# A fused attention and mixture-of-experts kernel: where the padding is awaited, how routing counts are kept, and where the residual is added

## The reference

```
x = layernorm(x + attn(x))                       # x: 1 x 2048 x 128
scores = x @ Wr + br                             # 8 experts
top 2 of scores; weights = softmax over these 2
out = sum over experts i of (relu(x @ W1[i] + b1[i]) @ W2[i] + b2[i]) * weight[i]
x = layernorm(x + out)                           # W1[i]: 128 x 512, W2[i]: 512 x 128
```

## Time and profile before

| what | us |
|---|---|
| median of 3 runs (lowest, highest) | 260.19 (259.41, 263.42) |
| the profiled execution | 259.66 |
| its span | 258.0 |
| busy: TensorE, VectorE, GpSimd, ScalarE | 183.3, 149.1, 119.6, 110.9 |

### The profile page before, as it was taken

How to read it: one execution, slowest core, us unless ns; L and a number is a source line. 1 busy time by engine, 2 the same in 40 slices (tenths; PEclk the granted TensorE clock), 3 DMA queues, 4 the chain that set the end, 5 groups by cost and what they waited for, 6 DMA issues and landing times.

```text
span 258.0 us, 5886 instructions
## 1 busy us (share of the span) xinstructions
PE 183.3 (71%) x1385; PEld 147.0 (57%) x1385; DVE 149.1 (58%) x546; ACT 110.9 (43%) x345; POOL 119.6 (46%) x188
## 2 busy tenths in 40 slices
PE   2999968609887899987420879897979798992000
PEld 1556425407565667655310879797969698892000
DVE  5489937007988857777660245554545445552393
ACT  1188774203556446665310224343424333450086
POOL 5000300041717636776776246666666636665360
PEclk9999995756999689999555599999999989998555
DMA  5999999995000101101113565666555656520743
GB/s 168 269 209 205 207 208 208 178 250 167 3 0 1 35 10 44 32 32 34 41 52 104 140 199 164 195 182 180 158 172 160 181 159 163 184 68 1 225 163 102
DMA packets 39554, 33.87 MB, mean 131 GB/s; under 512 B 3807, under 2 KB 33173, under 8 KB 39521
## 3 DMA queue, kind: packets, MB, share of 16 engines
q1 hardware_dynamic: 35264, 25.68, 45.2%
q0 software_dynamic: 3312, 7.64, 8.4%
q10 hardware_dynamic: 944, 0.17, 0.3%
HBM read 19.15 MB, written 14.79 MB: 132 GB/s over the span
## 4 chain that ended last, share of the span: by engine, by line
PE 24%; issue 11%; DVE 6%; POOL 5%; DMA 3%; ACT 2%; SPq 1%; POOLq 1%; DVEq 1%; ACTq 0%
PE psum L1337 11%; PE psum L1350 10%; POOL expert_results L534 3%; ACT x_sb L722 1%; PE psum L1325 1%; DMA xg<-expert_rows 1%; DMA gate<-expert_results 1%; DVE fstats L1101 1%; DVE xT L1098 1%; DMA expert_results<-kT,dest 1%; POOL dest L530 1%; DVE fshift L1093 1%; POOL expert_rows L490 0%; SPq L399 0%; PE psum L1239 0%
## 5 line engine op out<-in xcount | busy, mean ns | idle before, releaser
L534 POOL DMA_INDIRECT expert_results<-kT,dest x39 | 38.5, 987 | 37.4 <-issue 13.8
L1064 DVE TENSOR_SCALAR gT<-psum,b_sb 128x128 f32<-128x128 f32 x78 | 23.8, 346 | 35.9 <-PE psum L1337 23.3
L1350 PE MATMUL psum<-w_sb,gT 128*128 x312 | 43.8, 285 | 0.8 <-DVE gT L1064 0.8
L1350 PEld LDWEIGHTS psum<-w_sb,gT 128*128 128x128 f32 x312 | 39.2, 197 | 2.3 <-issue 1.4
L490 POOL DMA_INDIRECT expert_rows<-xr,slot x32 | 31.6, 986 | 13.4 <-issue 11.1
L699 ACT ACTIVATE gT<-psum,b_sb 128x128 f32<-128x128 f32 x78 | 24.4, 364 | 18.1 <-issue 15.1
L689 ACT ACTIVATE kT<-psum 128x128 f32<-128x128 f32 x39 | 10.8, 278 | 48.0 <-PE psum L1325 38.6
L1337 PE MATMUL psum<-kT,km 128*128 128x128 f32 x168 | 24.2, 292 | 9.1 <-issue 9.1
L1337 PEld LDWEIGHTS psum<-kT,km 128*128 128x128 f32 x168 | 22.0, 205 | 10.1 <-issue 10.1
L470 POOL TENSOR_TENSOR km<-kT,ek 128x512 f32<-128x512 f32 x4 | 5.1, 1282 | 46.7 <-ACT ek L593 24.5
L480 POOL TENSOR_TENSOR rgate<-rrms,gate 128x256 f32<-128x256 f32 x16 | 12.4, 776 | 21.1 <-ACT rrms L626 20.4
(11 more groups left out here) (170 smaller groups left out, 372.3 us busy)
## 6 DMA issues: line engine op xcount, KB each, us to landing
expert_rows<-pad_row SPq DMA_DIRECT2D x8, 1105.0 KB, 16.9
km<-in_L_ffn_W_dram SPq DMA_DIRECT2D x14, 256.0 KB
qm<-in_L_ffn_W_dram SPq DMA_DIRECT2D x12, 256.0 KB
xg<-expert_rows SPq DMA_DIRECT2D x39, 65.0 KB
gate<-expert_results SPq DMA_DIRECT2D x8, 256.0 KB, 4.2
km<-in_L_ffn_W_dram POOLq DMA_DIRECT2D x7, 256.0 KB
qm<-in_L_ffn_W_dram POOLq DMA_DIRECT2D x6, 256.0 KB
x_sb<-in_L_attn_x_dram SPq DMA_DIRECT2D x4, 256.0 KB, 4.3
```

Source lines behind the costliest of these rows:

```text
L534: pool.indirect_dma_start(out=results[:, :], in_=yw[:, u, :], in_offset=None, bounds_check=TOP * N - 1, oob_is_err=False, out_offset=bass. ...
L1064: dve.tensor_scalar(hT[:, h, HC // 2 + n, :], bank[2 * (i % 2) + 1][:, n * P:(n + 1) * P], b1_sb[:, bass.ds(e * HC + HC // 2 + n, 1)], 0.0 ...
L1350: last = mm(bank[4 + i % 2][:, 0:D], hT[:, h, n, :], w2_all[:, bass.ds(first + n * D, D)], start=(n == 0), stop=(n == HC - 1))
```

## The change

- The wait for the padding leaves the head of GpSimd's loop and stands before the first `scatter_rows`.
- GpSimd halves x (one instruction on 128 x 2048) once TensorE has transposed all of x; Wo is scaled by 0.5 too. The sum before the first layer norm is therefore half of what it was; its variance is multiplied by 4 before the inverse deviation is taken, so the normalized row comes out as half of x1. The half row is what is kept and scattered. ScalarE's copies for router and experts (`x1T`, `xgT`) scale by 2.
- Routing: `pile` holds, per batch, the running count and the four one-hots in bfloat16. The index-to-float cast, the add of hits, the second running sum, the score gap, the float-to-integer cast of places and the weight product on GpSimd are gone. The running count is one reduction per batch, the product stands on VectorE (`weigh`), the exponential takes the gap through its bias (two instructions per batch instead of one), places are picked and summed in the round in which they are taken, and `rank` issues six matrix products instead of two.
- Destinations are integers from the start, so GpSimd's cast in `scatter_results` is gone.
- `xg` has 8 buffers; the gather of slot i waits for the landed scatter of slot i-8, not for the weighting of slot i-6.
- The half row is added to the weighted output before it is scattered (L1077 becomes one instruction with two SBUF operands), so the end adds the two result rows on GpSimd alone. Result rows are loaded with 16 consecutive tokens per partition (2 KB pieces instead of 1 KB), output is stored in 1 KB pieces instead of 512 B. VectorE normalizes one tile of each pair, ScalarE the other.

```diff
-        top_f, hot, hit, so_far, gap, slot_f, dest = ...
+        pile = sb("pile", [P, NB + 1, 1 + 2 * TOP, E], BF16)
+        xg = sb("xg", [P, HELD, ROW])                       # HELD = 8
...
 def gather(i):                                              # SyncE
-                if i >= AHEAD:
-                    sp.wait_ge(s_yw, i - AHEAD + 1)
-                    sp.wait_ge(s_dest, i - AHEAD + 1)
+                if i >= HELD:
+                    sp.wait_ge(s_out[(i - HELD) % AHEAD], ((i - HELD) // AHEAD + 1) * 16)
...
+            pool.wait_ge(s_job, at["xT", NG - 1] + 1)
+            pool.tensor_scalar(x_sb[:, :, :], x_sb[:, :, :], 0.5, None, ALU.mult).then_inc(s_xhalf, 1)
...
-            pool.wait_ge(s_pad, 16 * E)
             pool.wait_ge(s_jact, n_act)
...
                 if b is not None:
-                    pool.wait_ge(s_w1st, b + 1)
-                    pool.tensor_tensor(xr[:, tt, 1, D], egap[:, tt], xr[:, tt, 0, D], ALU.mult).then_inc(s_weight, 1)
                     pool.wait_ge(s_slot, b + 1)
                     pool.wait_ge(s_weight, b + 1)
                     pool.wait_ge(s_xcopy, 2 * (b + 1))
+                    if b == 0:
+                        pool.wait_ge(s_pad, 16 * E)
...
 def scatter_results(i):                                     # GpSimd
-                pool.tensor_copy(dest[:, u:u + 1], xg[:, u, ROW - 1:ROW]).then_inc(s_dest, 1)
-                pool.wait_ge(s_dest, i + 1)
                 pool.wait_ge(s_yw, i + 1)
...
-                pool.tensor_tensor(acc[:, t, :], ysum[:, t, 0:D], xr[:, t, 0, 0:D], ALU.add).then_inc(s_acc0, 1)
+                pool.tensor_tensor(acc[:, t, :], ysum[:, t, 0:D], ysum[:, t, D:2 * D], ALU.add).then_inc(s_acc, 1)
...
 def exp_gap(b):                                             # ScalarE
-                act.activation(egap[:, tt], gap[:, tt], ACT.Exp).then_inc(s_egap, 1)
+                for t in (2 * b, 2 * b + 1):
+                    act.activation(egap[:, t:t + 1], top8[:, t, 0:1], ACT.Exp, bias=top8[:, t, 1:2], scale=-1.0).then_inc(s_egap, 1)
...
+            def count_hits(b):                              # VectorE
+                    dve.tensor_reduce(pile[:, b + 1, 0, :], pile[:, b, :, :].rearrange("p r e -> p e r"), AX_X, ALU.add).then_inc(s_sofar, 1)
+            def weigh(b):
+                dve.wait_ge(s_w1st, b + 1)
+                dve.tensor_tensor(xr[:, tt, 1, D], egap[:, tt], xr[:, tt, 0, D], ALU.mult).then_inc(s_weight, 1)
...
-                dve.tensor_scalar(yw[:, u, :], yb[:, h, :], xg[:, u, D:D + 1], None, ALU.mult).then_inc(s_yw, 1)
+                dve.scalar_tensor_tensor(yw[:, u, :], yb[:, h, :], xg[:, r, D:D + 1], xg[:, r, 0:D],
+                                         ALU.mult, ALU.add).then_inc(s_yw, 1)
...
+            def normalize_even(g):                          # VectorE; ScalarE keeps the odd tile
+                dve.scalar_tensor_tensor(fshift[:, g:g + 1], fmv[:, n + 1, 0:1], -1.0, frstd[:, n + 1:n + 2], ...)
+                dve.tensor_scalar(result[:, n, :], acc[:, n, :], fmv[:, n, 0:1], frstd[:, n:n + 1],
+                                  ALU.subtract, ALU.mult).then_inc(s_result_even, 1)
-                dve.tensor_tensor(acc[:, t, :], acc[:, t, :], ysum[:, t, D:2 * D], ALU.add).then_inc(s_acc, 1)
```

More of the change, by code:

```diff
@@ L274, in build @@
         s_table = sem("table_done")
-        s_xg = [sem(f"rows_gathered{u}") for u in range(AHEAD)]
+        s_xg = [sem(f"rows_gathered{u}") for u in range(HELD)]
         s_w1 = [sem(f"w1_gathered{u}") for u in range(AHEAD)]
@@ L930, in find_index @@
             def find_index(b):
-                tt = slice(2 * b, 2 * b + 2)
                 dve.wait_ge(s_top, 2 * b + 2)
@@ L934, in find_index, with one_hot @@
                     dve.max_index(top_at[:, t, :], top8[:, t, :], score[:, t, :]).then_inc(s_topat, 1)
[L935 to L937 removed]
+            def one_hot(b):
                 tt = slice(2 * b, 2 * b + 2)
                 dve.wait_ge(s_topat, 2 * b + 2)
[L940 to L958 removed]
+                dve.tensor_tensor(hot_of(b), expert_id[:, :].unsqueeze(1).unsqueeze(1).to_broadcast([P, 2, TOP, E]),
+                                  top_at[:, tt, 0:TOP].unsqueeze(3).to_broadcast([P, 2, TOP, E]), ALU.is_equal).then_inc(s_hot, 1)
+            def count_hits(b):
+                dve.wait_ge(s_hot, b + 1)
+                if b:
+                    dve.wait_ge(s_sofar, b)
+                with nc.allow_low_precision(reason="counts up to the number of tiles are exact"):
+                    dve.tensor_reduce(pile[:, b + 1, 0, :], pile[:, b, :, :].rearrange("p r e -> p e r"), AX_X, ALU.add).then_inc(s_sofar, 1)
+            def weigh(b):
+                tt = slice(2 * b, 2 * b + 2)
+                dve.wait_ge(s_w1st, b + 1)
+                dve.tensor_tensor(xr[:, tt, 1, D], egap[:, tt], xr[:, tt, 0, D], ALU.mult).then_inc(s_weight, 1)
             def take_places(b):
@@ L975, in sum_places @@
                 dve.wait_ge(s_placed, b + 1)
-                dve.tensor_reduce(slot_f[:, tt, :], placed[:, tt, :, :], AX_X, ALU.add).then_inc(s_slotf, 1)
-            def slots_to_int(b):
-                tt = slice(2 * b, 2 * b + 2)
-                dve.wait_ge(s_slotf, b + 1)
-                dve.tensor_copy(slot[:, tt, :], slot_f[:, tt, :]).then_inc(s_slot, 1)
+                with nc.allow_low_precision(reason="one whole number and zeros"):
+                    dve.tensor_reduce(slot[:, tt, :], placed[:, tt, :, :], AX_X, ALU.add).then_inc(s_slot, 1)
             dve.wait_ge(s_jact, n_act)
@@ L1246, in rank @@
             def rank(b):
-                pe.wait_ge(s_sofar, 2 * b + 2)
-                mm(bank[7][:, 400:400 + 2 * E], before_count[:, :], hit[:, 2 * b:2 * b + 2, :].rearrange("p t e -> p (t e)"),
-                   start=True, stop=False)
-                return mm(bank[7][:, 400:400 + 2 * E], ones_count[:, :], so_far[:, 2 * b:2 * b + 2, :].rearrange("p t e -> p (t e)"),
-                          start=False, stop=True)
+                pe.wait_ge(s_hot, b + 1)
+                if b:
+                    pe.wait_ge(s_sofar, b)
+                both = bank[7][:, 400:400 + 2 * E]
+                second = bank[7][:, 400 + E:400 + 2 * E]
+                for k in range(TOP):
+                    mm(both.rearrange("p (t e) -> p t e", e=E), before_count[:, :], hot_of(b)[:, :, k, :], start=(k == 0), stop=False,
+                       skip_group_check=True)
+                for t in range(2):
+                    mm(bank[7][:, 400 + t * E:400 + (t + 1) * E], ones_count[:, :], pile[:, b, 0, :], start=False, stop=(t == 0),
+                       skip_group_check=True)
+                for k in range(TOP):
+                    last = mm(second, ones_count[:, :], pile[:, b, 1 + k, :], start=False, stop=(k == TOP - 1), skip_group_check=True)
+                return last
             def attend(t):
```

145 lines of the change are left out of this document (59 added, 86 removed).

## The result

The changed kernel takes **242.07 us** (median of four runs, 240.64 to 242.11) against 260.7 in the same measurement (four runs, 259.41 to 263.42): a ratio of 0.929, 95% interval 0.923 to 0.935. The forecast was 243.3, the range 238 to 249. The profiled execution took 242.09 us, its span is 240.4. Throughout, a median is over all executions of a kernel, while a ratio and its interval use only those within 1.5% of its fastest, so the two need not agree to the last microsecond.

What follows compares the result with a forecast made beforehand. The kernel was taken as bound by TensorE with three idle holes. The terms 0.6 - 9.9 - 1.5 - 2.0 - 0.7 - 0.7 - 2.2 sum to -16.4, so 259.7 becomes 243.3 us; 8-in-10 range 238 to 249.

Steps and rivals of the forecast that it cites:

- The padding: TensorE's idle stretch before the output projection: 9.48 us goes, plus some clock gain; -9.9 us, ends 8.5 and 10.9.
- The halving: First stage: GpSimd's new instruction, taken as 3.1 us long, delays VectorE; +0.6 us, between 0 and 2.8.
- The rounds: Routing batches: VectorE loses five small instructions, gains `weigh`, TensorE gets more matmuls; -1.5 us, ends -4 and +1.5.
- The scatter chain and the second hole: TensorE's idle in slices 20 to 22: without GpSimd's weight products, slot 2's W1 is issued earlier; -2.0 us.
- The experts: Expert slots: without the cast, lagging scatters start about 0.5 us earlier and the last two gaps shrink; -0.7 us.
- my rival: Expert slots: the cast made GpSimd late for W1, so six gaps lose half, 3 us more; chance 0.17.
- The tail: Last result scatter: it begins 0.81 us behind the last weighting instead of 1.56; -0.7 us.
- The end: Final normalization: VectorE's pace gains 1.4 us, ScalarE's work behind the last statistics 0.8; -2.2 us, ends -3.5 and 0.
- the rival: End: VectorE's normalization is held beside GpSimd's adds, five groups at up to 0.4, 2.0 us, eating the gain; chance 0.18.
- Only the padding: Whole kernel: only the padding counts, as VectorE's savings lie beside a busy TensorE; 249 us, chance 0.18.
- The gaps close as well: Experts: six W1 gaps lose half, 3 us more, and with 2 from the rounds 238.5 us; chance 0.17.
- Slower by gathers that wait for landed scatters: Experts: slot i's gather waits for a landed scatter, a loss if landing takes over 3.9 us; 265 or more, chance 0.02.

Runs made afterwards that it cites:

- W1 first: The changed kernel with GpSimd issuing the W1 load of slot i+5 ahead of the scatter of slot i instead of behind it: 236.58 us, ratio 0.908.
- the product back: The changed kernel with the product of the two routing weights back on GpSimd ahead of each batch's scatters: 243.90 us, ratio 0.937.
- the end back: The changed kernel with both tiles of each of the eight end groups normalized on ScalarE, as before: 240.26 us, ratio 0.926.
- both parts together: The changed kernel without the halving of x on GpSimd and with W1's load issued ahead of the scatter: 236.00 us, ratio 0.902.
- the padding alone: The kernel before with the padding wait moved to the first row scatter and nothing else: 252.51 us beside 261.75.

## Why the prediction was right, step by step

*The padding* (-9.9): -9.5, and the mechanism as told: GpSimd took the keys up 11.6 us earlier, and no wait for the padding is left in its list. The half microsecond for the clock didn't come in this trace: the four matmuls took 1.23 us, still at 1.2 GHz. It came in others. Where the granted clock had risen to 0.83 to 1.00 just before the first residual (the changed kernel's second trace and those of W1 first, the product back, the end back, and both parts together), first scores to first residual takes 9.2 to 10.8 us; where it was still 0.50 (this trace and four more, the padding alone among them) 12.3 to 13.7. The means are 10.2 and 12.9. If the clock is all that parts the two groups, which was not tried, it gives back 2.7 us and not 0.5, and the padding's removal is then worth 11.5, beyond my upper end of 10.9. That the pair of traces came within 0.4 of my term is in part luck. That the padding's landing itself moves by 3.7 us between traces was in no bound.

*The halving* (+0.6): the step that was mis-sized. I chose the length by the count of operands, from the affine select, 3.1 us; it took 5.38, my upper end (5.3), 2.6 ns a column, as with two operands. The Trainium skill (GPSIMD Engine Reference, Engine selection), by which one input is roughly line-rate there, an estimate of 1.7 us, doesn't hold for this instruction. The delay of VectorE was then 1.2 and not 2.8, because my second assumption failed as well: the product began at 15.07, was done at 16.93, and GpSimd went on to 18.10; the scan behind it took its usual 1.23. So two errors, one in each direction. With 0.2 us by which the input was later (x transposed at 12.53, 12.34 before) and 0.2 more on the way, the first scores came 1.5 later.

*The rounds* (-1.5): -3.7 in the two traces, but that isn't the routing's price. The windows of the rounds (us, TensorE busy (instructions), its weight loads, VectorE, ScalarE, GpSimd, then mean granted clock, DMA share, GB/s), one fence for each kernel: before; changed; changed with the end on ScalarE; before with the padding moved.

```profile
59.87:124.91 65.04, 56.16 (x523) 40.51 (x522) 50.56 (x219) 35.71 (x134) 36.68 (x43) 0.92 0.09 29
```

```profile
51.93:113.30 61.37, 53.96 (x547) 39.73 (x546) 46.43 (x194) 36.85 (x140) 35.33 (x39) 0.94 0.23 65
```

```profile
49.88:109.33 59.45, 51.22 (x547) 37.41 (x545) 45.78 (x195) 36.98 (x142) 36.04 (x39) 1.00 0.33 76
```

```profile
50.69:112.26 61.57, 52.43 (x523) 37.65 (x522) 51.02 (x219) 35.71 (x134) 36.26 (x43) 0.99 0.33 76
```

The same rounds' code took from 59.45 us at a mean clock of 1.00 to 63.8 at 0.87 to 0.89 (three traces). The clock is not all of it: the old rounds took 65.04 us at 0.92 and 64.03 at 0.90. At like clock, old routing against new: 61.57 against 59.45 (0.99 and 1.00), 65.04 against 61.55 (0.92 both), 64.03 against 63.79 (0.90 and 0.89). That is -0.2 to -3.5, middle -2.1, with VectorE's busy time 4.1 to 5.2 less and 24 more matmuls on record. At full clock the difference can be seen directly: residuals two tiles apart stand 7.91 us apart in the old routing (82.22 to 90.13 with the padding moved) and 7.52 in the new (84.71 to 92.23 in the changed kernel). So the term was right within what can be told: 0.2 to 3.5 of the -3.7 is the routing's, and what is left, 1.6 by the middle pair, is put down to the clock and not measured apart.

*The scatter chain and the second hole* (-2.0): -1.7, and 1.4 of it is the product's move, by one pair of traces. What I had for VectorE's side, a wait of `weigh` for ScalarE's weight, is there (0.6 us in the table's chain).

*The experts* (-0.7): -1.5. The mechanism I named, lagging scatters without their copy, is worth 1.2 by one pair of traces, 1 to 2 by all. The form that I gave it failed: the last gaps did not shrink; that before slot 35 grew to 2.68. VectorE's fused multiply-add took 0.35 us and not the 0.29 that I had by its operand size. GpSimd issued this W1 at 202.78, 5.8 us ahead of its use, where such loads landed 3.1 us after their issue at the median and 5.1 at most; what held this one up I haven't found. Four other traces with the same order have a gap of 1.7 to 2.2 there, three have 0.5 or less. And the largest cause of the gaps was in neither my terms nor my rival, which had seen the gaps and put them down to the cast: it is the order of load and scatter, untouched by the change and worth 2 to 5 us in it.

*The tail* (-0.7): -0.6, from 1.85 to 1.25.

*The end* (-2.2): -2.2 in the pair of traces, -2.4 in the means. The shares were off: I gave the split 0.8 behind the last statistics and a part of the pace, and it has at most 0.5 in all. One reason can be seen: VectorE's normalization is held in the groups that run beside GpSimd's additions (0.79 to 0.86 in three groups against 0.34), as the rival said. It ate a part, not the whole.

**The rivals.** Only the padding (249): fallen, as the rest is worth 7.7 by itself. The gaps close as well (238.5): they shrank, from 8.0 to 5.7 us in all from slot 8 on, but did not close, and taking the load ahead of the scatter closed them. Slower by gathers that wait for landed scatters: after the first slots TensorE has no wait for gathered rows in the changed kernel. That the sum came within 1.2 us owes something to errors that cancel: the halving and the padding cost 1.3 more than I had, and the rounds and the experts gave 3.0 more. Luck has a part in it too, since the same stretches move by 3 us and more between traces.

## What to carry to other kernels

Put a wait at the first instruction that needs it, and on an engine that runs its queue in order ask what each wait holds up behind it: here it was worth 9 to 12 of 18.6 us, and a load queued behind a scatter another 2 to 5 in the changed kernel, though only 1 to 2 in the total of the kernel before. Before a scaling is given to an idle engine, see whether an operation that runs anyway can take the factor; the fused addition cost nothing, while the idle engine's instruction stopped another one. When a term is read off two traces, set the granted clock of the stretch beside it and ask how far the stretch moves in traces of the same code: here the same rounds took 65.04 us at 0.92 and 61.57 at 0.99.

## What the hardware did that I had not expected

- GpSimd's one-operand product over 128 x 2048 took 5.38 us in all eight traces that have it, 2.6 ns a column, the same per column as its two-operand product over 512 (1.33 us in the earlier trace rows).
- What it does to VectorE depends on the instruction. A scale of 128 x 256 of SBUF data that began 0.06 us behind it went from 0.33 to 5.47 us, its whole length. A fused product of 128 x 512 that began 2.35 behind went from 0.68 to 1.86 and was done 1.17 before GpSimd was; a scan beside the rest was not slowed (1.23). The Trainium skill (SBUF — State Buffer, Who interferes with whom) has an exclusive lock on the shared ports; the first case agrees with it, the second shows that not every VectorE instruction is locked out to the end. Another product of VectorE on 128 x 512 (`qc`, L802 in the kernel before) took 1.64 us beside GpSimd's key product at 30.27 and 0.69 at 42.51, when GpSimd stood idle. What decides was not tried.
- The clock: in the changed kernel the output projection's four matmuls took 0.71 us at 67.82 (granted clock 1.00, 2.4 GHz), 1.23 at 74.25 (0.50, 1.2 GHz), after TensorE had stood idle for 0.51 and 1.33 us in between, and 0.71 again at 79.96. In two other traces of nearly the same code the granted clock was 1.00 through all rounds.
- The padding, 8.84 MB on one queue from 5.8 us on, was waited for until 55.04 us in one trace and until 58.62 and 58.75 in two others.
